# Fewer semaphore increments in the sort of a graph kernel: cell counts signalled in pairs and units, rank one-hots three groups ahead, carries released by the products

## What is computed

```python
src_h = h[src] @ W_msg.T + b_msg
msg = src_h + edge_embed[edge_type]
messages = segment_sum(msg, dst, num_segments=num_nodes)
h_new = gru_cell(messages, h, W_ih, W_hh, b_ih, b_hh)
x = layernorm(x + h_new)
agg = segment_sum(concat([h[src], edge_attr @ enc_w + enc_b]), dst)   # three layers
x = layernorm(x + mlps(agg))
```

## Time and profile before

| what | value |
|---|---|
| median of three runs | 9094.97 us |
| the profiled execution's own time | 9098.04 us |
| its span, first to last instruction | 9096.2 us |
| PE busy, of the span | 6077.8 us (67%) |
| DVE busy | 3476.6 us (38%) |
| ACT busy | 1489.0 us (16%) |
| POOL busy | 4775.4 us (52%) |
| mean granted TensorE clock | 0.824 |

### The profile page before, as it was taken

One profiled execution on the slowest core, in us unless ns is written; L12 is line 12 of the kernel. 1 busy time (PEld: TensorE's weight loads), 2 busy tenths in 40 slices (PEclk: granted clock), 3 DMA queues, 4 the chain that ended last, 5 costly groups with the idle time before them and its releaser, 6 DMA issues. The chain is left out here.

```text
span 9096.2 us, 88724 instructions
## 1 busy us (share of the span) xinstructions
PE 6077.8 (67%) x28807; PEld 2856.9 (31%) x28807; DVE 3476.6 (38%) x14291; ACT 1489.0 (16%) x2862; POOL 4775.4 (52%) x4959
## 2 busy tenths in 40 slices
PE   3354546454554533555555799899898988888888
PEld 1122212121221211232223344444344444344343
DVE  7354535354453533344434444444221212222222
ACT  1122212132222311111112222222000000000000
POOL 5543343434434354544453566666666666666664
PEclk9876767676776766766667899999999999999999
DMA  6265646475665654322222677777776777776775
GB/s 205 57 146 123 155 110 164 111 175 125 161 143 137 157 129 101 83 73 76 77 80 67 199 230 216 220 229 228 222 215 200 223 213 212 233 207 204 208 212 177
DMA packets 1390704, 1478.16 MB, mean 163 GB/s; under 512 B 818695, under 2 KB 1131926, under 8 KB 1390246
## 3 DMA queue, kind: packets, MB, share of 16 engines
q1 hardware_dynamic: 1177750, 1123.36, 43.7%
q0 software_dynamic: 212496, 349.08, 15.2%
HBM read 1024.47 MB, written 280.48 MB: 143 GB/s over the span
## 5 line engine op out<-in xcount | busy, mean ns | idle before, releaser
L2768 POOL DMA_INDIRECT GL<-h_gathered,IDXA x2646 | 2562.0, 968 | 1529.4 <-issue 703.5
L2690 PE MATMUL ps<-MS,HP 128*128 128x512 bf16 (+1 forms) x11700 | 2829.4, 385 | 84.1 <-issue 58.3
L2735 POOL DMA_INDIRECT rec_q<-BIG x1563 | 1503.6, 962 | 1999.6 <-DVE BIG L1821 1505.5
L2475 PE MATMUL ps<-MT,XPS 128*128 128x512 bf16 x3822 | 1173.3, 421 | 1307.4 <-issue 931.6
L2690 PEld LDWEIGHTS ps<-MS,HP 128*128 128x128 bf16 x11700 | 1160.8, 101 | 1397.1 <-issue 323.8
L2253 ACT CAST MT<-ps 128x512 bf16<-128x512 f32 x1274 | 736.4, 586 | 2466.3 <-remote 1320.1
L2750 POOL DMA_INDIRECT BIG<-x_parts,SRCq x739 | 704.8, 954 | 740.7 <-PE ps L2572 452.3
L2475 PEld LDWEIGHTS ps<-MT,XPS 128*128 128x128 bf16 x3822 | 381.6, 104 | 1886.7 <-issue 1121.6
L2081 DVE TENSOR_REDUCE ROW<-ps 128x128 f32<-128x384 f32 x294 | 163.0, 554 | 1740.0 <-remote 858.6
L1871 DVE CAST CAR<-ps 128x98 f16<-128x98 f32 x429 | 109.2, 255 | 1722.5 <-remote 1343.7
L2660 PE MATMUL ps<-GL,SL 128*128 128x384 bf16 (+1 forms) x2646 | 613.5, 341 | 37.5 <-issue 37.0
(11 more groups left out here) (225 smaller groups left out, 4959.3 us busy)
## 6 DMA issues: line engine op xcount, KB each, us to landing
MS<-counts SPq DMA_DIRECT2D x936, 512.0 KB
counts<-BIG SPq DMA_DIRECT2D x312, 512.0 KB
XPS<-x_parts SPq DMA_DIRECT2D x168, 384.0 KB
GL<-h_gathered,IDXA POOLq DMA_INDIRECT x2646
rec_q<-BIG POOLq DMA_INDIRECT x1563
rec_q<-BIG SPq DMA_DIRECT2D x44, 490.0 KB, 10.9
HTI<-h_cols SPq DMA_DIRECT2D x72, 256.0 KB
RECL<-rec_q SPq DMA_DIRECT2D x24, 520.0 KB
```

Of the source, the lines that this page charges most:

```text
L2475: got = t.matmul(PS[6 + x.j % 2][:, :], XPS[:, x.load % 3, i, part, :], MT[:, m % 3, 512 * i:512 * (i + 1)], start=4 * x.u + i + part == 0 ...
L2690: got = t.matmul(bank[:, 0:w].rearrange("p (b c) -> p b c", c=P), HP[:, d, part, :], MS[:, i % MR, 0:x.nb, d % MB, :], start=d + part == 0 ...
L2735: g.indirect_dma_start(out=RAd, out_offset=bass.IndirectOffsetOnAxis(ap=POSI[:, c:c + 1], axis=0), in_=RECA[q % 3][:, c - a, :], in_offset ...
L2768: g.indirect_dma_start(out=GL[:, r % LR, i, 0:3 * P], out_offset=None, in_=HGd[lay], in_offset=bass.IndirectOffsetOnAxis(ap=IDXA[:, a + i: ...
```

## The change

Eight things, all in the sort.

- `mt` (PE, a cell made) is raised once for two cells, on the second matmul of a pair; `mt_out` (ACT, a cell copied) once for two copies; `xd` (PE, cell times x) once a unit.
- `ohs` and `ohd` become one semaphore, `made`, raised once a unit, behind its last `OHD`. PE waits for it before the first cell of the unit.
- PE makes two cells one behind the other and then the sums of two cells, where it made one of each in turn.
- `OH` has four buffers instead of three; `rank_onehot` runs three groups ahead of the step instead of two, and only the first three groups raise `hot` and are waited for.
- `car` is gone: PE's carry matmul waits for `prod`, which is raised by the instruction after the copy of the carry.
- Reduces raise DVE's own semaphore only where a piece's places follow, and `mk` in `window_places` doesn't raise it.
- The waits of the other engines' programs, and of the DMA queue, are restated in pairs and units.
- Arithmetic, tiles, DMAs and the order of the steps stay as they are.

```diff
@@ buffers and semaphores
-        OH = [big(GT * NB // 2).bitcast(F16).rearrange("p (c b) -> p c b", b=NB) for _ in range(3)]
+        OH = [big(GT * NB // 2).bitcast(F16).rearrange("p (c b) -> p c b", b=NB) for _ in range(4)]
-        car = sem("rank_carries")
-        ohs = sem("cell_src")
-        ohd = sem("cell_dst")
+        made = sem("cell_onehots")
@@ window_places, rank_onehot, cells_vector, sort_vector (DVE)
-            v.scalar_tensor_tensor(mk, r, float(128 if w.dense else 128 * K), mk, ALU.is_le, ALU.mult).then_inc(*dve.inc())
+            v.scalar_tensor_tensor(mk, r, float(128 if w.dense else 128 * K), mk, ALU.is_le, ALU.mult)
...
-            if g >= 3:
-                v.wait_ge(rank.sem, g - 2)
+            if g >= 4:
+                v.wait_ge(rank.sem, g - 3)
             for c in range(GT):
                 at = GT * i + c
-                got = v.tensor_scalar(OH[g % 3][:, c, :], IOTM[:, :, 0:NB // 7], KEY[w.q % 2][:, at:at + 1], None, ALU.is_equal)
-            got.then_inc(*hot.inc())
+                got = v.tensor_scalar(OH[g % 4][:, c, :], IOTM[:, :, 0:NB // 7], KEY[w.q % 2][:, at:at + 1], None, ALU.is_equal)
+            if g < 3:
+                got.then_inc(*hot.inc())
...
             if m >= 3:
-                v.wait_ge(mt.sem, cells_to(m - 3))
+                v.wait_ge(mt.sem, cells_to(m - 3) // 2)
             for i in range(x.n):
-                got = v.tensor_scalar(OHS[m % 3][:, i, :], I132[:, :, 0:44], RECS[k % 2][:, par, x.at + i, 1:2], None, ALU.is_equal)
-            got.then_inc(*ohs.inc())
+                v.tensor_scalar(OHS[m % 3][:, i, :], I132[:, :, 0:44], RECS[k % 2][:, par, x.at + i, 1:2], None, ALU.is_equal)
             for i in range(x.n):
                 c = x.c0 + i
-                if c >= 8:
-                    v.wait_ge(mt.sem, c - 7)
-                v.tensor_scalar(OHD[c % 8], I516[:, :, 0:172], DSF[k % 2][:, par, x.at + i:x.at + i + 1], None,
-                                ALU.is_equal).then_inc(*ohd.inc())
+                if c >= 8 and c % 2 == 0:
+                    v.wait_ge(mt.sem, c // 2 - 3)
+                got = v.tensor_scalar(OHD[c % 8], I516[:, :, 0:172], DSF[k % 2][:, par, x.at + i:x.at + i + 1], None, ALU.is_equal)
+            got.then_inc(*made.inc())
 
         def sort_vector(v):
             window_keys(v, WIN[0])
-            rank_onehot(v, WIN[0], 0)
-            rank_onehot(v, WIN[0], 1)
+            for i in range(3):
...
                     v.wait_ge(rank.sem, g + 1)
-                    if CARRY[g][0]:
-                        v.tensor_copy(CAR[:, g % 2, :], PS[g % 2][:, (GT - 1) * NB:GT * NB]).then_inc(*car.inc())
+                    if CARRY[g]:
+                        v.tensor_copy(CAR[:, g % 2, :], PS[g % 2][:, (GT - 1) * NB:GT * NB])
                     v.tensor_tensor(PRD[g % 2], PS[g % 2][:, 0:GT * NB].rearrange("p (c b) -> p c b", b=NB),
-                                    OH[g % 3][:, :, :], ALU.mult).then_inc(*prod.inc())
-                    if i + 2 < w.groups:
-                        rank_onehot(v, w, i + 2)
+                                    OH[g % 4][:, :, :], ALU.mult).then_inc(*prod.inc())
+                    if i + 3 < w.groups:
+                        rank_onehot(v, w, i + 3)
                     elif w.q < 24:
-                        rank_onehot(v, WIN[w.q + 1], i + 2 - w.groups)
+                        rank_onehot(v, WIN[w.q + 1], i + 3 - w.groups)
                     if w.q == 0 and 1 <= i < 7:
                         keys_vector(v, i - 1)
                     for m in UNIT_AT[g]:
                         cells_vector(v, m)
                     v.wait_ge(prod.sem, g + 1)
-                    v.tensor_reduce(RNK[w.q % 2][:, GT * i:GT * i + GT], PRD[g % 2], X, ALU.add).then_inc(*dve.inc())
+                    got = v.tensor_reduce(RNK[w.q % 2][:, GT * i:GT * i + GT], PRD[g % 2], X, ALU.add)
                     for x in PIECES:
                         if x.w is w and x.b == GT * (i + 1):
+                            got.then_inc(*dve.inc())
                             window_places(v, x)
@@ cells_scalar (ACT)
-                s.wait_ge(xd.sem, cells_to(m - 3))
+                s.wait_ge(xd.sem, m - 2)
             for i in range(x.n):
                 c = x.c0 + i
-                s.wait_ge(mt.sem, c + 1)
-                s.copy(MT[:, m % 3, 512 * i:512 * (i + 1)], PS[2 + c % 4][:, :]).then_inc(*mt_out.inc())
+                if c % 2 == 0:
+                    s.wait_ge(mt.sem, c // 2 + 1)
+                got = s.copy(MT[:, m % 3, 512 * i:512 * (i + 1)], PS[2 + c % 4][:, :])
+                if c % 2 == 1:
+                    got.then_inc(*mt_out.inc())
@@ ranks_tensor, cells_tensor, sums_tensor (PE)
-            oh = OH[g % 3]
-            t.wait_ge(hot.sem, g + 1)
+            oh = OH[g % 4]
+            if g < 3:
+                t.wait_ge(hot.sem, g + 1)
...
-                t.wait_ge(car.sem, CARRY[g - 1][1])
+                t.wait_ge(prod.sem, g)
...
             x = UNITS[m]
-            t.wait_ge(ohs.sem, m + 1)
-            for i in range(x.n):
+            t.wait_ge(made.sem, m + 1)
+            for i in range(0, x.n, 2):
                 c = x.c0 + i
-                t.wait_ge(ohd.sem, c + 1)
                 if c >= 4:
-                    t.wait_ge(mt_out.sem, c - 3)
-                t.matmul(PS[2 + c % 4][:, :], OHS[m % 3][:, i, 0:P], OHD[c % 8][:, 0:512], start=True, stop=True).then_inc(*mt.inc())
+                    t.wait_ge(mt_out.sem, c // 2 - 1)
+                t.matmul(PS[2 + c % 4][:, :], OHS[m % 3][:, i, 0:P], OHD[c % 8][:, 0:512], start=True, stop=True)
+                t.matmul(PS[3 + c % 4][:, :], OHS[m % 3][:, i + 1, 0:P], OHD[(c + 1) % 8][:, 0:512], start=True, stop=True).then_inc(*mt.inc())
                 if c >= 2:
                     sums_tensor(t, c - 2)
+                    sums_tensor(t, c - 1)
...
-            t.wait_ge(mt_out.sem, c + 1)
+            t.wait_ge(mt_out.sem, c // 2 + 1)
...
-            got.then_inc(*xd.inc())
+            if i == x.n - 1:
+                got.then_inc(*xd.inc())
@@ cells_sync (DMA queue)
-            y.wait_ge(mt_out.sem, cells_to(m))
+            y.wait_ge(mt_out.sem, cells_to(m) // 2)
```

More of the change, by code:

```diff
@@ L148, in carries @@
 def carries():
-    on, n = [], 0
+    on = []
     for w in WIN:
         for i in range(w.groups):
-            last = i == w.groups - 1 and (w.q + 1 >= 25 or WIN[w.q + 1].fresh)
-            n += 0 if last else 1
-            on.append((not last, n))
+            on.append(not (i == w.groups - 1 and (w.q + 1 >= 25 or WIN[w.q + 1].fresh)))
     return on
@@ L1837, in cells_vector @@
                 if k >= 2:
-                    v.wait_ge(ohd.sem, cells_to(last_unit(lambda y: y.half == k - 2)))
+                    v.wait_ge(made.sem, last_unit(lambda y: y.half == k - 2) + 1)
                 w = 4 * HU if k % 2 == 0 else NB - 4 * HU
@@ L1844, in cells_vector @@
             if m >= 3:
-                v.wait_ge(mt.sem, cells_to(m - 3))
+                v.wait_ge(mt.sem, cells_to(m - 3) // 2)
             for i in range(x.n):
-                got = v.tensor_scalar(OHS[m % 3][:, i, :], I132[:, :, 0:44], RECS[k % 2][:, par, x.at + i, 1:2], None, ALU.is_equal)
-            got.then_inc(*ohs.inc())
+                v.tensor_scalar(OHS[m % 3][:, i, :], I132[:, :, 0:44], RECS[k % 2][:, par, x.at + i, 1:2], None, ALU.is_equal)
             for i in range(x.n):
                 c = x.c0 + i
-                if c >= 8:
-                    v.wait_ge(mt.sem, c - 7)
-                v.tensor_scalar(OHD[c % 8], I516[:, :, 0:172], DSF[k % 2][:, par, x.at + i:x.at + i + 1], None,
-                                ALU.is_equal).then_inc(*ohd.inc())
+                if c >= 8 and c % 2 == 0:
+                    v.wait_ge(mt.sem, c // 2 - 3)
+                got = v.tensor_scalar(OHD[c % 8], I516[:, :, 0:172], DSF[k % 2][:, par, x.at + i:x.at + i + 1], None, ALU.is_equal)
+            got.then_inc(*made.inc())
         def sort_vector(v):
             window_keys(v, WIN[0])
-            rank_onehot(v, WIN[0], 0)
-            rank_onehot(v, WIN[0], 1)
+            for i in range(3):
+                rank_onehot(v, WIN[0], i)
             for w in WIN:
@@ L2258, in sums_scalar @@
         def sums_scalar(s, j):
-            s.wait_ge(xd.sem, cells_to(last_unit(lambda y: y.j == j)))
+            s.wait_ge(xd.sem, last_unit(lambda y: y.j == j) + 1)
             if j >= 2:
@@ L2498, in weights_tensor @@
             t.wait_ge(weights_dve.sem, 8)
-            t.wait_ge(mt_out.sem, len(CELLS))
+            t.wait_ge(mt_out.sem, len(CELLS) // 2)
             t.wait_ge(acc_out.sem, JX)
-            t.wait_ge(car.sem, CARRY[-1][1])
+            t.wait_ge(prod.sem, NG)
             for i in range(2):
@@ L2788, in cell_records_sync @@
             if k >= 2:
-                y.wait_ge(ohs.sem, last_unit(lambda z: z.half == k - 2) + 1)
+                y.wait_ge(made.sem, last_unit(lambda z: z.half == k - 2) + 1)
```

(2 more changed lines are left out.)

## The result

The changed kernel takes 9134.17 us, median of 15 runs (9103.93 to 9145.66). The kernel before takes 9086.99 us beside it, also over 15 runs (9059.53 to 9102.18). The ratio is 1.0048, 95% interval 1.0037 to 1.006: slower by 44 us by the ratio and by 47 us by the medians. The forecast was 33 us.

A forecast was written before the change was run, and what follows sets the result against it. Waits bound the sort, a chain of scatter, remaining ranks and cells, places, next scatter. 9098.0 (profiled execution) + 32.5 = 9130.5; that execution is 3.1 us over the median, so 9128 us, range 9050 to 9180.

The forecast's parts named there:

- What bounds the kernel: Sort stage with cells: no engine is full; a chain of scatter, remaining ranks and cells, places, next scatter, every 140 to 159 us.
- A scatter of more than 75: Sign on POOL's scatters: the forecast is wrong if one holds more than 75 PE matmuls; 60 to 67 were expected.
- Matmuls, not increments, have the price in a scatter: PE during scatters: 2.7 to 2.9 us a matmul, nothing for an increment, so dropping increments there gains 0.
- The rival in which increments are slow: PE in scatters: increments are what is slow, copies come under 9 us apart, 9046 us (or 9084); chance 0.21.
- Increments between scatters: PE between scatters: increments cost 0; the rival that they hold PE back gains 25 us, 9103 us, chance 0.05.
- The handoff `made`: Between scatters, windows 4 to 12: PE starts a unit 1.12 us later, and DVE's wait for the rank grows as much.
- The term 29 x 1.12 = 32.5: Windows 4 to 12: of 34 PE waits before a unit, 29 delay DVE's rank by 1.12 us each, 32.5 us.
- Windows 13 to 24: Windows 13 to 23 in the prediction: units are made before PE comes, DVE's 4.10 us a step covers it, unchanged, 0.
- Pairs, carries on products, one-hots three ahead: Cells copied in pairs, PE's carry matmul waiting for the product, one-hots one group earlier: each put at 0.
- The step on the carry: PE's carry matmul starts at 1393.54 instead of 1393.06, before PE's 2 us of idle time: 0, uncovered 0.48 us a group.
- The handoff absorbed: Units that PE starts late run without a break or get the clock sooner; all 32.5 us gone, 9095 us, chance 0.16.
- the rival with the clock: PE's longer idle time before 29 units brings one more clock dip each, 1.7 us: +49 us, 9177 us, chance 0.09.

The follow-up runs named there:

- 3: The kernel before with 2991 more increments on PE's matmuls, on a semaphore nobody waits for: 9212.68 us, ratio 0.9997 to the kernel before.
- 10: The kernel before with one sums matmul of a cell instead of three, so not the reference's result: 9009.14 us, ratio 0.9789.
- 2: The kernel before with one edit, PE waits for a unit's last destination one-hot before its first cell: 9264.43 us, ratio 1.0050.
- 1: The changed kernel with `made` raised once for two cells instead of once a unit: 9220.89 us, ratio 1.0005 to the kernel before.
- 4: The kernel before with a unit's cell one-hots written ahead of the next rank's one-hots: 9163.6 us, ratio 0.9949.
- 9: The changed kernel again, unedited, on another chip with slow completions: 9245.08 us, ratio 1.0051 to the kernel before.
- experiment 11: The kernel before with each window's scatter cut in two, the first part written while the window is still being ranked: 9036.24 us, ratio 0.9827.

## Why the prediction was right, step by step

**What bounds the kernel.** As put: scatter, rest of the window, places, next scatter. POOL's wait for places grew by 40 us and the sort with it. Over all 21 full scatters the kernel before has 52 to 77 matmuls in one, 65 on average, and the changed one 53 to 82, 66 on average; the 60 to 67 of the prediction was its two rows. A scatter of more than 75 was to be a sign of being wrong, and there is one of 82. The kernel before already has one of 77 and the averages agree, so the sign was set too close; the regime is the same.

**Matmuls, not increments, have the price in a scatter.** Shown by 3 and 10, and in the changed kernel itself. Its copies come in pairs there (x2 in the rows):

```profile
2087.49 1.07 ACT L2251 CAST MT<-ps 128x512 bf16<-128x512 f32 x2 [17.62 <-remote]
2109.12 1.07 ACT L2251 CAST MT<-ps 128x512 bf16<-128x512 f32 x2 [20.55 <-remote]
```

From 2087.49 to 2109.12 it is 21.6 us for eight matmuls, 2.7 each, and it is one increment on `mt` and at most one on `xd` where two cells had four. The rival in which increments are slow asked for under 9 us a cell; it is 10.8, and that rival is out.

**Increments between scatters.** 0, as put. The Trainium skill, TensorE: Matmul & The Clock Gate, section "The cost: per-tile semaphore tail", gives increments on matmuls some 26 ns each, one after another. By it experiment 3 would have been 78 us slower (2991 x 0.026, an estimate) and it was not: its interval ends at 1.0012, 11 us. On these 128 x 512 matmuls the measurement decides, and that rival is out too.

**The handoff `made`.** The mechanism and its place are shown by three runs on either side: alone it brings the loss (2), at half its grain most of the loss goes (1), and the same way shortened instead brings a gain (4). The size for one turn, 1.12 us, is what the close-up shows, 1.12 for PE's start and 1.14 for the two steps. The term 29 x 1.12 = 32.5 was too small; measured are 45.7 us. Its count was nearly right for what it counted: 28 steps with a unit grew between scatters. Two things were missing. The steps without a unit have a price of their own, 11.6 us: the prediction looked only at places where PE is seen to wait, and PE is late for a unit without that too. And a turn is not always 1.12: the steps with a unit come to 38.0 us, with single steps up to 2.99, and the prediction had put the clock at nothing in its sum. The steps inside scatters, put at 0, came out at -3.9.

**Windows 13 to 24** were to stay, and did, within 1.8 us. The reason given, that the unit is already made when PE comes to it and DVE's 4.10 us a step are the bound, agrees with that; no run tested it by itself.

**Pairs, carries on products, one-hots three ahead.** All were put at 0. Experiment 1, which has all of them with a finer `made`, leaves at most 20 us for their sum and the pairwise handoff together (1.0022). Experiment 2, which has none of them, comes out like the changed kernel (1.0050 and 1.0048). Each alone was not tried. The step on the carry missed one thing that does not change the sum: its 0.48 us later start takes that much out of PE's wait in front of the unit, so that this wait is 0.64 us longer, not the 1 us given as a sign.

**The handoff absorbed, or aggravated by the clock.** In the turn of the close-up neither is seen. PE starts at the higher of its two clock levels (its first matmuls are 0.22 us apart), falls to the lower (six sums at 1432.81 take 2.76 us) and comes back (six at 1436.21 take 1.46). From the first cell to the rank behind the unit it is 1437.51 - 1432.36 = 5.15 us, and it was 1400.54 - 1395.41 = 5.13, with a stretch at the lower level as well. Over the 34 units in front of which PE waits between scatters (over 1.5 us each, in the trace before) it is not always so. At the higher level that time is 3.45 us, and over 5.4 us it takes in 2 of the 34 before and in 4 in experiment 3, but in 10, 12 and 10 of them in the three traces with a coarse wait (after, 9 and 2). So the rival with the clock, which had 9177 us for one more dip at each of 29 turns, has a part in the loss. How large it is stays open: the 34 times sum to 157.9 and 143.9 us in the two kernels with the fine wait, and to 173.8, 169.1 and 158.5 us in the three with the coarse one. Nothing shows the handoff absorbed.

## What to carry to other kernels

Where two engines take turns, the grain of a semaphore is part of the path: its price here was the work that the producer does between the first item and the last, about once for each turn, and more where the waiting engine came back at a lower clock. A list of the consumer's waits does not give the number of turns: of the nine steps without a unit that grew, eight had none of PE's listed in front of their rank. Lay the two traces beside each other step by step for that. Where the unit was made before the consumer came to it (windows 13 to 24) the same coarsening cost nothing, and the increments saved gave nothing back; look for the stretches in which the consumer comes first before thinning a signal. And an engine whose wait grows need not be the one that the edit touched: here DVE's wait for ranks showed the 44 us that a semaphore from DVE to PE had cost.

## What the runs showed of the hardware

- While POOL scatters rows to HBM by indirect DMA, one column in 1.26 us, PE's completions come at 2.7 to 2.9 us a matmul, with cells and sums alone (10.8 / 4) or with a rank group among them (26.2 / 9), and with two increments in four matmuls or four (experiment 3). By an estimate from experiment 11, 31 to 41 matmuls get through before that sets in. After the scatter PE is back at 0.215 us a matmul. What slows it was not found.
- It depends on the chip. On one the same kernel takes 6570 us instead of 9087 to 9212, and PE does 326 matmuls in the same 80 us. Why was not found.
- Scatters cut in two gave 159 us on a chip with slow completions, at an unchanged total of 1563 columns, and on the other chip the ratio was 0.9989 (0.9979 to 0.9998). The allowance at the start of each scatter explains it, but that is argued: no run separates it from the earlier start of the first part. Finer cuts were not tried.
